# Turned attention probabilities kept tile by tile, and value matmuls that read them with a stride of 16 words

## The chip, the core and the metric

The kernel runs on one core of one Trainium2 chip. Its time is the device time of one launch in microseconds (us). The engines are TensorE (PE in the rows, its weight loads PEld), VectorE (DVE), ScalarE (ACT), GpSimd (POOL) and SyncE (SP), which issues the DMAs. SBUF has 128 partitions; PSUM is used here as eight banks of 128 partitions x 512 fp32 words.

## The reference, cut to what matters

The program is a network of eight blocks over 4 sequences (lanes) of 512 tokens and 128 features: windowed and linear attention, experts, two attentions with relative positions, two windowed attentions with rotary positions and a long convolution. The change touches the two attentions with relative positions alone. With 16 heads of 8 features they compute, for each lane:

```
att = q.k^T * scale + q.rk          (rk: a row of embk that depends on the distance t - s)
att = softmax(att)                   (the first attention is causal, the second is not)
y   = att @ v  +  einsum('bhts,tsd->bhtd', att, rv)
```

Each probability is so used twice: against the values `v` of its head, and against a table `rv` that depends on the distance alone.

## The kernel before, in words

All else being untouched, what counts is `core(s)`, written once for each engine, and run twice: `which` 0 (causal, about 775 to 1185 us of the span) and `which` 1 (not causal, about 1395 to 2085 us).

The unit of work is a tile: 8 queries (`QG`) of 16 heads (`HEADS_R`), 128 rows in order (query, head), against `nk` blocks of 128 keys. `nk` is 4 in the second attention, and 1 to 4 in the first (block of the query plus 1). There are 256 tiles in each attention, 16 tiles (one block of 128 queries) make a batch. All engines walk in steps of two tiles (`core_steps`), each part of the work at its own lag: scores at lag 6, turn at 8, embedded at 10, chosen at 12. So what a step makes is used by PE one step later, except the scores, whose softmax is used by the turn one step later as well.

For a tile:

- `scores` (PE): five or six matmuls into a bank, rows (query, head), columns keys. They are of type fp32r.
- `maxima` (DVE), `exps` (ACT), `normal` (DVE): the softmax, written to `PR`, rows (query, head).
- `turn` (PE, line 937): `nk` transposes to a bank, now rows keys, columns (block, query, head).
- `turned` (ACT, in the rows line 1166, the helper `copy`): the bank to `PT` in SBUF. `PT` has 3 slots of 8 tiles (`t.slot`); in a slot the order of words is (block, head, 64 queries), and a tile fills 8 queries in each head (`t.cols`). The copy reads its bank in order and writes word after word 64 words apart.
- `embedded` (PE): the probabilities of a tile against the table by distance, weights of 64 columns, the moving side a tile's 128 words of `PT`: 16 runs of 8 words, 64 words apart. Two matmuls run side by side, in two halves of the array's columns.
- `chosen` (DVE, line 1554): from the bank of `embedded` the words that belong to each own query, into `WB`, in order (head, query).
- `values` (PE): for a batch and each block, weights of 32 columns from `VS`, the moving side 2 slots x 64 queries of one head, in `PT` two runs of 64 words in order. Four matmuls run side by side, in four strips of the array's columns, each with another head. They are spread over 8 of the 16 tiles of a later batch.
- `fold` (PE) adds what `chosen` left, and `head_copy` (DVE) brings the batch out.

In the rows `low` is the memory that holds `PR`, `PT` and `VS`; `bank<-low` with weights of 128*32 is `values`, `bank<-low,table_low` with 128*64 is `embedded`; `halves`, `table_keys` and `exact` are operands of `scores`; `slot` holds `WB` and one of the four `PR`. Line 730 is the helper `mm`.

Of the kernel before, what the change touches and what calls it, by code (L numbers as in the profile page):

```python
# [22 lines left out]
P = 128  # L23
C = 4
T = 512
NT = T // P
# [9 lines left out]
HEADS_R, D_R, QG = 16, 8, 8  # L36
# [399 lines left out]
def hybrid_network(nc, ins, scratch, out):  # L436
    plan, released, bank_of, tile_before = make_plan()
    ctx = ExitStack()
    with ctx:
# [5 lines left out]
        def sem(name):  # L445
            if name not in sems:
                sems[name] = ctx.enter_context(nc.semaphore(name))
            return sems[name]

        bank = [ctx.enter_context(nc.psum_tensor(f"bank{b}", [P, T], F32)) for b in range(BANKS)]  # L450
# [26 lines left out]
        def carve(*shape):  # L477

            size = 1
            for s in shape:  # L480
                size *= s
            a = place[0][:, cursor[0]:cursor[0] + size]
            cursor[0] += size
            assert cursor[0] <= place[1], cursor[0]
            if len(shape) == 1:
                return a
            names = "abcd"[:len(shape)]
            return a.rearrange(f"p ({' '.join(names)}) -> p {' '.join(names)}",
                               **{n: s for n, s in zip(names[1:], shape[1:])})
# [35 lines left out]
        PR3 = carve(3, T)  # L525
        NBR, RSR, RIR = carve(4), carve(8), carve(8)
        VS = carve(NT, 4, 4, 32)
        PT = carve(3, NT, HEADS_R, QG * QG)
        cursor[0], place = 0, [halves, WORK_W - LOW]
        A4, AX4 = carve(2, 2, T), carve(2, 2, T)  # L530
        B4 = carve(2, T)
# [9 lines left out]
        WB = slots[1][:, WR_W:WR_W + 2 * HEADS_R * QG * QG].rearrange("p (a h q) -> p a h q", a=2, h=HEADS_R)  # L541
# [29 lines left out]
        def k_(name):  # L571
            a, w = CONST[name]
            return const[:, a:a + w]
# [34 lines left out]
        def reached(eng, name, count):  # L608

            if not isinstance(count, int) or count > 0:  # L610
                eng.wait_ge(sem(name), count)

        def score_columns(t):

            return t.nk * P if t.which or t.g < 4 else (t.nk - 1) * P + (t.g + 1) * QG

        def core_steps(which):

            for T_ in range(0, STEPS, 2):
                def st(work_, lag, T_=T_):
                    if 0 <= T_ - lag < TILES:
                        work_(Tile(which, T_ - lag))
                yield T_, st
# [93 lines left out]
        def _(pe):  # L721
# [7 lines left out]
            def mm(o, l, r, start=True, stop=True):  # L729
                return pe.matmul(o, l, r, start=start, stop=stop)  # L730
# [156 lines left out]
            def core(s):  # L887
# [52 lines left out]
                def embedded(t):  # L940
                    pe.wait_ge(sem("r_turn_copied"), t.at + 1)
                    reached(pe, "r_chosen", t.at - 1)
                    o = bank[4 + t.G % 2]
                    near = list(range(t.nk)) if s.which else [t.block - 1, t.block]
                    for j, b in enumerate(near):
                        apart = b - t.block
                        if b < 0:
                            rows_ = k_("zeros")
                        elif apart < -1:
                            rows_ = far_before  # L950
                        elif apart > 1:
                            rows_ = far_after
                        else:
                            first = (P * (apart + 1) + P - QG - QG * t.g) * D_R
                            rows_ = value_table[:, first:first + QG * D_R]
                        strip = slice(64 * (j % 2), 64 * (j % 2) + 64)
                        last = mm(o[strip, 0:P], rows_, PT[:, t.slot, max(b, 0), :, t.cols], start=(j < 2), stop=(j + 2 >= len(near)))
                    last.then_inc(sem("r_embedded"), 1)

                def values(T_):  # L960
                    k, part = divmod(T_ - VALUES, BATCH)
                    if not (0 <= k < BATCHES and part < QG):
                        return
                    lane, block = divmod(k, NT)
                    nk = NT if s.which else block + 1
                    two = sorted((2 * k % 3, (2 * k + 1) % 3))
                    moving = PT[:, two[0]:two[1] + 1:two[1] - two[0]]
                    steps = [(b, i) for b in range(nk) for i in range(4)]
                    if part == 0:
                        pe.wait_ge(sem("r_values_spread"), 4 * (C * s.which + lane) + 4)  # L970
                        reached(pe, "r_head_copied", BATCHES * s.which + k)
                    for b, i in steps[-(-part * len(steps) // QG):-(-(part + 1) * len(steps) // QG)]:
                        for strip in range(4):
                            last = mm(bank[7][32 * strip:32 * strip + 32, 0:P], VS[:, b, strip, i, :], moving[:, :, b, 4 * strip + i, :],
                                      start=((b, i) == steps[0]), stop=((b, i) == steps[-1]))
                        if (b, i) == steps[-1]:
                            last.then_inc(sem("r_values"), 1)
# [23 lines left out]
                for T_, st in core_steps(s.which):  # L1001
                    st(scores, SCORES)
                    st(scores, SCORES - 1)
                    st(spread, SCORES - 2)
                    st(turn, TURN)
                    st(turn, TURN - 1)
                    st(embedded, EMBED)
                    st(embedded, EMBED - 1)
                    values(T_)
                    values(T_ + 1)  # L1010
                    fold(T_)
# [148 lines left out]
        def _(act):  # L1160
# [4 lines left out]
            def copy(dst, src):  # L1165
                return act.activation(dst, src, ACT.Identity)  # L1166
# [71 lines left out]
            def core(s):  # L1238
                def turned(t):
                    act.wait_ge(sem("r_turned"), t.at + 1)  # L1240
                    m = t.G // QG
                    if t.G % QG == 0 and m >= 3:
                        act.wait_ge(sem("r_values"), BATCHES * s.which + (m - 3) // 2 + 1)
                    copy(PT[:, t.slot, 0:t.nk, :, t.cols].rearrange("p b h q -> p b q h"),
                         bank[2 + t.G % 2][:, 0:t.nk * P].rearrange("p (b q h) -> p b q h", b=t.nk, q=QG))\
                        .then_inc(sem("r_turn_copied"), 1)

                def exps(t):
                    act.wait_ge(sem("r_max"), t.at + 1)
                    n = score_columns(t)  # L1250
                    act.activation(PR[t.G % 4][:, 0:n], bank[t.G % 2][:, 0:n], ACT.Exp, bias=NBR[:, t.G % 4:t.G % 4 + 1],  # L1251
                                   accum_out=RSR[:, t.G % 8:t.G % 8 + 1]).then_inc(sem("r_exp"), 1)

                for T_, st in core_steps(s.which):
                    st(exps, SCORES)
                    st(exps, SCORES - 1)
                    st(turned, TURN)
                    st(turned, TURN - 1)
# [80 lines left out]
        def _(dve):  # L1339
# [201 lines left out]
            def core(s):  # L1541
# [7 lines left out]
                def chosen(t):  # L1549
                    half = t.G // QG % 2  # L1550
                    dve.wait_ge(sem("r_embedded"), t.at + 1)
                    if t.G % QG == 0:
                        reached(dve, "r_folded", 2 * BATCHES * s.which + 2 * (t.batch - 1) + half + 1 if t.batch else 0)
                    dve.tensor_tensor(WB[:, half, :, t.cols], bank[4 + t.G % 2][:, 0:P].rearrange("p (h q) -> p h q", h=HEADS_R),  # L1554
                                      k_("own_query").rearrange("p (h q) -> p h q", h=HEADS_R), ALU.mult)\
                        .then_inc(sem("r_chosen"), 1)

# [43 lines left out]
                for T_, st in core_steps(s.which):  # L1601
                    st(chosen, CHOSEN)
                    st(chosen, CHOSEN - 1)
                    position_copy(T_)
                    head_copy(T_)
                    st(maxima, SCORES)
                    st(maxima, SCORES - 1)
                    st(normal, SCORES)
                    st(diagonal, SCORES - 2)
                    st(normal, SCORES - 1)  # L1610
# [349 lines left out]
```

## Time and profile before

| what | value |
|---|---|
| median of 3 runs | 3362.26 us (3359.34 to 3362.66) |
| profiled execution, its own time | 3348.03 us |
| its span | 3346.1 us |
| mean granted TensorE clock | 0.963 |
| PE busy (matmuls) | 3069.0 us, 92% |
| DVE busy | 2030.3 us, 61% |
| ACT busy | 1893.0 us, 57% |
| POOL busy | 773.8 us, 23% |

The busy share of PE counts a matmul to its modelled end, and matmuls overlap, so it is not a measure of what the array can do. The pace of PE is read from how many instructions lie in a stretch, and its idle time from the view of waits.

### The profile page before, as it was taken

The numbers are of one execution on the slowest core, as the hardware profiler recorded it, in microseconds if no ns is written. First come the engines' busy times: TensorE is split into PE (matmuls) and PEld (weight loads), VectorE is DVE, ScalarE is ACT, GpSimd is POOL, SyncE is SP. The second block draws the span as 40 slices with busy tenths as digits, with TensorE's granted clock in tenths as the row PEclk, the third lists the DMA queues.
The fourth block names the chain that finished last, engine by engine and source line by source line (L and its number), as shares of the span: only waits on it lengthen the run. The fifth ranks groups of instructions, "written<-read, shape, count | busy, mean of one in ns | idle before, by whom it ended". The sixth has DMA issues, their size and how long they took to land. (4 is left out here: it accounts for less than half of the span.)

```text
span 3346.1 us, 61245 instructions
## 1 busy us (share of the span) xinstructions
PE 3069.0 (92%) x22620; PEld 2079.8 (62%) x22620; DVE 2030.3 (61%) x6331; ACT 1893.0 (57%) x4388; POOL 773.8 (23%) x683
## 2 busy tenths in 40 slices
PE   8999999978999998799999999888888998888888
PEld 6666667546888885488888887344344463443444
DVE  5454535366677675666666666667566425774765
ACT  5464656514666663266666665666565615665665
POOL 1000000102233230244444442221222012212220
PEclk9898999988999998899999999899999999999999
DMA  1010000000000001000000000210111002111110
GB/s 48 1 37 1 11 1 8 1 4 8 2 2 2 2 2 30 21 2 2 2 1 2 2 2 28 88 39 20 41 39 29 20 1 58 38 27 27 41 36 13
DMA packets 34537, 61.57 MB, mean 18 GB/s; under 512 B 11182, under 2 KB 15302, under 8 KB 33094
## 3 DMA queue, kind: packets, MB, share of 16 engines
q1 hardware_dynamic: 34246, 57.65, 6.3%
q8 instruction: 187, 3.06, 0.4%
q14 instruction: 104, 0.85, 0.1%
HBM read 21.97 MB, written 1.11 MB: 7 GB/s over the span
## 5 line engine op out<-in xcount | busy, mean ns | idle before, releaser
L730 PE MATMUL bank<-work 128*64 128x128 f32 (+8 forms) x4992 | 581.5, 302 | 65.5 <-DVE work L1649 36.0
L730 PEld LDWEIGHTS bank<-work 128*64 128x64 f32 (+3 forms) x4992 | 426.1, 165 | 261.6 <-issue 162.9
L1569 DVE TENSOR_REDUCE low<-bank 128x1 f32<-128x512 f32 (+22 forms) x512 | 293.6, 574 | 294.8 <-PE bank L730 293.1
L1251 ACT ACTIVATE low<-bank,low 128x512 f32<-128x512 f32 (+23 forms) x384 | 227.9, 594 | 395.9 <-DVE low L1569 394.9
L1166 ACT ACTIVATE low<-bank 128x512 f32<-128x512 f32 (+3 forms) x512 | 424.0, 938 | 0.9 <-PE bank L937 0.9
L730 PE MATMUL bank<-table_keys,halves 128*128 128x512 f32 (+3 forms) x1536 | 418.2, 381 | 0.2 <-ACT low L1251 0.2
L1283 ACT ACTIVATE work<-work 128x192 f32<-128x192 f32 (+1 forms) x512 | 221.4, 436 | 263.9 <-DVE work L1636 263.4
L1166 ACT ACTIVATE work<-bank 128x512 f32<-128x512 f32 (+4 forms) x469 | 262.0, 577 | 137.2 <-PE bank L730 54.2
L1796 POOL TENSOR_TENSOR work<-work 128x512 f32<-128x512 f32 x128 | 164.0, 1281 | 595.5 <-DMA work<-work 593.7
L730 PEld LDWEIGHTS bank<-table_keys,halves 128*128 128x128 f32 x1536 | 253.2, 192 | 68.6 <-issue 34.6
L730 PE MATMUL bank<-halves 128*128 128x512 f32 (+3 forms) x1024 | 286.8, 362 | 1.0 <-DVE halves L1562 0.9
L1757 POOL TENSOR_TENSOR halves<-squared,const 128x512 fp32r<-128x512 f32 x128 | 135.6, 1059 | 650.1 <-PE bank L730 650.1
L1717 POOL TENSOR_SCALAR normed<-normed,slot 128x512 f32<-128x512 f32 x48 | 78.6, 1637 | 736.2 <-DVE normed L1394 735.9
L730 PE MATMUL bank<-work,slot 128*128 128x512 f32 x408 | 198.7, 622 | 34.1 <-ACT work L1166 29.2
L730 PE MATMUL bank<-low,table_low 128*64 128x128 f32 x2944 | 225.0, 281 | 0.3 <-DVE slot L1554 0.3
L1170 ACT ACTIVATE squared<-centered 128x512 f32<-128x512 f32 x80 | 50.1, 630 | 287.7 <-DVE centered L1387 287.6
L730 PE MATMUL bank<-normed,slot 128*128 128x512 f32 x440 | 206.8, 613 | 1.7 <-POOL normed L1717 1.7
L730 PE MATMUL bank<-centered,const 128*128 128x512 f32 x256 | 146.9, 656 | 65.9 <-ACT centered L1264 65.1
L730 PEld LDWEIGHTS bank<-halves 128*128 128x128 f32 x1024 | 184.9, 191 | 31.3 <-DVE halves L1562 3.2
L1547 DVE TENSOR_SCALAR low<-low 128x512 f32<-128x512 f32 (+23 forms) x384 | 191.2, 498 | 13.6
L1049 PEld LDWEIGHTS bank<-const,work 128*128 128x128 f32 x896 | 111.6, 145 | 127.8 <-issue 104.1
L730 PEld LDWEIGHTS bank<-low,table_low 128*64 128x64 f32 x2944 | 162.9, 136 | 38.0 <-issue 37.9
(182 smaller groups left out, 5601.7 us busy)
## 6 DMA issues: line engine op xcount, KB each, us to landing
work<-work SPq DMA_DIRECT2D x512, 64.0 KB, 2.0
slot<-in_wW SPq DMA_DIRECT2D x4, 1605.5 KB, 7.0
slot<-in_wA SPq DMA_DIRECT2D x4, 837.0 KB, 6.3
table_low<-embv_padded SPq DMA_DIRECT2D x2, 1536.0 KB, 6.3
table<-in_dft SPq DMA_DIRECT2D x1, 3072.0 KB, 11.7
slot<-in_wE SPq DMA_DIRECT2D x2, 584.0 KB, 3.7
const<-in_const SPq DMA_DIRECT2D x1, 1094.0 KB, 5.1
squared<-in_x SPq DMA_DIRECT2D x4, 256.0 KB, 6.2
```

The costliest lines, as they stand in the source:

```text
L730: return pe.matmul(o, l, r, start=start, stop=stop)
L1049: last = pe.transpose(o[:, (2 * a + blk) * P:(2 * a + blk + 1) * P], PW[:, s.n % 3, a, blk * P:(blk + 1) * P], ident)
L1166: return act.activation(dst, src, ACT.Identity)
L1170: act.activation(squared[:, s.c, :], centered[:, s.c, :], ACT.Square).then_inc(sem("norm_squared"), 1)
L1251: act.activation(PR[t.G % 4][:, 0:n], bank[t.G % 2][:, 0:n], ACT.Exp, bias=NBR[:, t.G % 4:t.G % 4 + 1], accum_out=RSR[:, t.G % 8:t.G % 8 + ...
L1283: last = act.activation(PW[:, s.n % 3, a, lo:256], SW[:, s.n % 2, a, lo:256], ACT.Exp, scale=-1.0, bias=small_w[:, s.n % 4, a:a + 1], accu ...
L1547: dve.tensor_scalar(row, row, inverse, None, ALU.mult).then_inc(sem("r_normal"), 1)
L1569: dve.tensor_reduce(out=NBR[:, t.G % 4:t.G % 4 + 1], in_=bank[t.G % 2][:, 0:score_columns(t)], axis=AX.X, op=ALU.max, negate=True).then_in ...
L1717: pool.tensor_scalar(a, a, wt(s, s.table, s.gain[1]), None, ALU.add).then_inc(sem("norm_done"), 1)
L1757: pool.tensor_tensor(A4[:, half, Q % 2, :].rearrange("p (t h) -> p t h", h=HEADS_R), bc(one_lane.unsqueeze(2), [P, 4 * QG, HEADS_R]), bc(k ...
L1796: pool.tensor_tensor(R1[:, s.n % 3, :], R1[:, s.n % 3, :], R2[:, s.n % 3, :], ALU.add).then_inc(sem("w_added"), 1)
```

## The change

`PT` is laid out anew: a slot is now (tile of the 8, block, 128 words as the turn gives them, in order (query, head)). The ACT copy thus reads and writes in order. `embedded` reads 128 words in order, and its result comes in order (query, head), so `chosen` reads its bank with a stride of 16 words and writes `WB` as before. `values` needs one head of 2 x 64 queries: it reads 128 words that lie 16 words apart (in 8 tiles for each slot, 8 words each). The sizes of all operands, the waits and the order of the instructions on each engine stay as they were.

```diff
-        PT = carve(3, NT, HEADS_R, QG * QG)
+        PT = carve(3, QG, NT, P)
...
-                        last = mm(o[strip, 0:P], rows_, PT[:, t.slot, max(b, 0), :, t.cols], start=(j < 2), stop=(j + 2 >= len(near)))
+                        last = mm(o[strip, 0:P], rows_, PT[:, t.slot, t.G % QG, max(b, 0), :], start=(j < 2), stop=(j + 2 >= len(near)))
...
-                    moving = PT[:, two[0]:two[1] + 1:two[1] - two[0]]
+                    slots_ = slice(two[0], two[1] + 1, two[1] - two[0])
...
-                            last = mm(bank[7][32 * strip:32 * strip + 32, 0:P], VS[:, b, strip, i, :], moving[:, :, b, 4 * strip + i, :],
+                            last = mm(bank[7][32 * strip:32 * strip + 32, 0:P], VS[:, b, strip, i, :], PT[:, slots_, :, b, 4 * strip + i:P:HEADS_R],
...
-                    copy(PT[:, t.slot, 0:t.nk, :, t.cols].rearrange("p b h q -> p b q h"),
-                         bank[2 + t.G % 2][:, 0:t.nk * P].rearrange("p (b q h) -> p b q h", b=t.nk, q=QG))\
+                    copy(PT[:, t.slot, t.G % QG, 0:t.nk, :].rearrange("p b f -> p (b f)"), bank[2 + t.G % 2][:, 0:t.nk * P])\
...
-                    dve.tensor_tensor(WB[:, half, :, t.cols], bank[4 + t.G % 2][:, 0:P].rearrange("p (h q) -> p h q", h=HEADS_R),
+                    dve.tensor_tensor(WB[:, half, :, t.cols], bank[4 + t.G % 2][:, 0:P].rearrange("p (q h) -> p h q", h=HEADS_R),
                                       k_("own_query").rearrange("p (h q) -> p h q", h=HEADS_R), ALU.mult)\
```

## Rows read from the trace of the kernel before

**Rows 1.** The page, busy time of each engine

```profile
PE 3069.0 (92%) x22620; PEld 2079.8 (62%) x22620; DVE 2030.3 (61%) x6331; ACT 1893.0 (57%) x4388; POOL 773.8 (23%) x683
```

**Rows 2.** Windows: stretch, its us, busy time of each engine, granted clock

```profile
920.00:1046.00 126.00, 125.77 (x1466) 106.03 (x1460) 89.14 (x288) 77.76 (x198) 36.48 (x37) 1.00 0.01 2
1570.00:1740.00 170.00, 170.00 (x1895) 138.77 (x1894) 114.31 (x311) 111.08 (x193) 80.81 (x70) 1.00 0.01 2
```

**Rows 3.** PE's waits from 1395 to 2085 us: total, times, longest

```profile
PE bank L730 <- POOL halves L1757: 11.4, 1, 11.4
PE bank L937 <- ACT low L1166: 1.0, 2, 0.7
PE bank L730 <- DVE centered L1598: 0.5, 1, 0.5
PE bank L730 <- ACT low L1251: 0.2, 1, 0.2
```

**Rows 4.** Timeline of a steady stretch: start, us, engine, operation [idle before]

```profile
1701.71 0.85 PE L730 MATMUL bank<-table_keys,halves 128*128 128x512 f32 x3
1701.91 0.69 DVE L1569 TENSOR_REDUCE low<-bank 128x1 f32<-128x512 f32 x1 [0.63 <-PE bank L730]
...
1702.40 0.62 PE L730 MATMUL bank<-halves 128*128 128x512 f32 x2
1702.63 0.42 PEld L730 LDWEIGHTS bank<-halves,exact 128*128 128x128 f32 x2
1702.63 0.69 ACT L1251 ACTIVATE low<-bank,low 128x512 f32<-128x512 f32 x1 [0.57 <-DVE low L1569]
1702.86 0.63 PE L730 MATMUL bank<-halves,exact 128*128 128x512 f32 x2
...
1703.33 1.04 PE L937 MATMUL bank<-const,low 128*128 128x128 f32 x8
...
1704.29 1.09 PE L730 MATMUL bank<-low,table_low 128*64 128x128 f32 x16
...
1704.46 1.98 ACT L1166 ACTIVATE low<-bank 128x512 f32<-128x512 f32 x2
```

**Rows 5.** Groups by form, ACT's copies: count | busy us, mean ns | idle

```profile
L1166 ACT ACTIVATE low<-bank 128x512 f32<-128x512 f32 x320 | 319.7, 1110 | 0.0
...
L1166 ACT ACTIVATE low<-bank 128x384 f32<-128x384 f32 x64 | 49.8, 887 | 0.0
L1166 ACT ACTIVATE work<-bank 128x512 f32<-128x512 f32 x345 | 196.5, 590 | 56.2 <-PE bank L1121 30.6 <-PE bank L827 11.6 <-PE bank L1049 7.7
L1166 ACT ACTIVATE low<-bank 128x256 f32<-128x256 f32 x64 | 34.8, 652 | 0.0
L1166 ACT ACTIVATE low<-bank 128x128 f32<-128x128 f32 x64 | 19.7, 413 | 0.9 <-PE bank L937 0.9
...
L1166 ACT ACTIVATE work<-bank 128x256 f32<-128x256 f32 x16 | 5.8, 360 | 0.0
```

**Rows 6.** Line 1166: who waited for its copies, us and times

```profile
  PE bank L937: 2.4, 4
```

**Rows 7.** Timeline of the second attention's end

```profile
2075.28 3.78 ACT L1166 ACTIVATE low<-bank 128x512 f32<-128x512 f32 x4
2075.41 0.16 DVE L1546 RECIPROCAL low<-low 128x1 f32<-128x1 f32 x1 [0.25 <-ACT slot L1251]
2075.61 0.49 DVE L1547 TENSOR_SCALAR slot<-slot,low 128x512 f32<-128x512 f32 x1
...
2076.46 0.63 PE L937 MATMUL bank<-const,low 128*128 128x128 f32 x4 [0.72 <-ACT low L1166]
...
2077.35 0.63 PE L937 MATMUL bank<-const,slot 128*128 128x128 f32 x4 [0.26 <-ACT low L1166]
...
2077.91 2.24 PE L730 MATMUL bank<-low,table_low 128*64 128x128 f32 x32
...
2080.07 1.96 PE L730 MATMUL bank<-low 128*32 128x128 f32 x64
```

**Rows 8.** Line 730, matmuls of values: count, ns min/median/max

```profile
L730 PE MATMUL bank<-low x3328: 272/273/298, 815.2 to 2083.9; 128*32 128x128 f32 x196
```

**Rows 9.** Groups by form, DVE from 780 to 2090 us

```profile
L1554 DVE TENSOR_TENSOR slot<-bank,const 128x128 f32<-128x128 f32 x512 | 123.0, 279 | 5.4 <-PE bank L730 4.8
...
L1596 DVE COPY centered<-bank 128x128 f32<-128x128 f32 x11 | 3.1, 283 | 5.5 <-PE bank L730 5.5
```

## The prediction

> **What bounds the kernel now.** I read the page first: PE is busy for 92% of the span, ACT for 57% [rows 1]. That is a mean over stages, so the windows come next, of the two stages that the change touches. In a steady stretch of the second attention PE is busy for 170.00 of 170.00 us, DVE for 114.31, ACT for 111.08; in the first attention (920 to 1046 us) it is 125.77, 89.14 and 77.76 of 126 [rows 2]. PE's clock is granted in full (2.4 GHz) in both. A busy PE could still be one that overlaps modelled ends with small waits, so I look at its waits: in the whole second attention it waits 11.4 us once for POOL at the start, and 1.7 us in all beside that, 1.0 us of it for the ACT copies that the change makes shorter [rows 3]. The reader is to see that no line of these is a wait in the steady part. So in both attentions the time is the sum of what PE's instructions take, and ACT and DVE run beside it with a third of their time idle.
>
> The timeline of a step shows that this holds by a wide margin. The copies of a step's turned tiles run from 1704.46 to 1706.44 [rows 4], and their reader (`embedded` at lag 10) comes one step later, some five us on. DVE idles 0.63 us before the first maximum, ACT 0.57 us before the exponential [rows 4].
>
> **The ACT copies.** There are 512: 320 of 512 words at 1110 ns, and 64 each of 384, 256 and 128 words at 887, 652 and 413 ns [rows 5]. The same helper with both sides in order takes 590 ns for 512 words and 360 ns for 256 (two runs of 128) [rows 5]. That is 0.90 ns a word, and by it 475 ns for 384 and 245 ns for 128. The saving on ACT is 320 x 0.520 + 64 x (0.412 + 0.292 + 0.168) = 166 + 56 = 222 us. It is large, and nearly all of it lies beside PE. On the path lies only what PE waits for: 2.4 us in four places over both attentions [rows 6]. At the end of the second the timeline tells why. No more scores come, PE has little to do, and the turn needs the bank that the copy of two tiles before still reads: 0.72 and 0.26 us [rows 7]. Four copies in a row take 3.78 us there, with 590 ns each about 2.4; the last turn then starts near 2076.5 instead of 2077.35. I take 1 us for each attention, 2 us in all, from 0 to 2.5.
>
> **`embedded`.** It reads 128 words in order in place of 16 runs of 8. Sixteen instructions, in eight pairs, take 1.09 us, so the pairs follow each other in (1.09 - 0.27)/7 = 0.117 us, where 0.27 is the length of the last. The eight transposes, which read 128 words in order, one at a time, take 1.04 us, (1.04 - 0.27)/7 = 0.110 us [rows 4]. The pace is nearly the same, so runs of 8 cost little or nothing before. Were the rest of 7 x 0.007 = 0.05 us due to them, 256 steps of two tiles would give back 13 us. But it can as well be the wait for the first weights of a new width, as `values`, in order, also starts with 0.113 for 0.110 (below). I take 0, from 0 to -13.
>
> **`chosen`.** 512 DVE instructions of 279 ns [rows 9] now read their bank with a stride of 16 words. A plain copy of the same size with both sides in order takes 283 ns [rows 9], so the runs of 8 that it writes cost nothing today; the strided read is not in the trace. If each of the 128 words cost as much more as ACT's strided writes do (next part: 0.92 ns), one would take 0.12 us longer, 0.24 us in a step of two tiles; the 0.63 us of idle time before the next maximum [rows 4] covers it. Behind it on DVE are the maximum, the reciprocal and the scaling, and PE needs those one step later. I take 0; below it nothing is to be had, and with the cover gone at every step it would be 256 x 0.24 = 61 us, which I hold for very unlikely since the turn has the better part of a step of slack.
>
> **`values`.** This alone is on PE's own path. There are 3328 instructions [rows 8], four side by side, so 832 rounds of 128 words for each strip. From the row of 64 (16 rounds) in 1.96 us [rows 7]: (1.96 - 0.27)/15 = 0.113 us a round, 94 us over both attentions. After the change each stream takes a word from a new place at every step. No matmul of this kernel does that today, so I bound it from both sides.
> - Below: reading in order is no slower than anything else of this type here, so there is no gain; 0.
> - For free: PE's reading has room. The fp32r matmuls of `scores` start at 1701.71 and the sixth at 1702.86 [rows 4], 0.230 us for 512 words, 0.45 ns a word. The fp32 matmuls take 0.113/128 = 0.88 ns a word. So the stream that is to be strided runs at half of the pace that the same engine reaches in order, and a penalty of up to two would be hidden.
> - Like ACT: its writes with 64 words between them cost (1110 - 413)/384 = 1.82 ns a word, in order (590 - 360)/256 = 0.90 [rows 5]. If PE's read paid 1.82 ns too, a round would take 128 x 1.82 = 0.233 us, 0.120 more: 832 x 0.120 = +100 us.
> - The far end: four streams read side by side. If what they share hands out several neighbouring words at once, words in order need one fetch for four, and strided words one fetch each. A round would take four times as long, 0.339 us more: +282 us.
>
> I take the free case, 0, for `values`: the row of fp32r is of the same engine and the same side (a read), that of ACT is a write by another engine.
>
> The Trainium skill speaks against this change. SBUF — State Buffer, on cachelines in its part on the ports, says that SBUF has lines of 16 bytes, that two accesses to a line are needed for full bandwidth, and that each access to a new line pays a penalty; here every word is on a line of its own. What the penalty is it does not say. The doubled cost of ACT's strided words agrees with it. No row shows a strided read by PE. If the penalty is a halving of the best pace of the engine, an estimate from that rule and the fp32r rows is 0.90 ns a word, 2 us in all, and the sum stays; if it is a fixed time for each line it is rival 1.
>
> **Sum.** -2 (ends) + 0 + 0 + 0 = -2 us. In the profiled execution 3348.0 becomes 3346.0; the median of the runs, 14 us above it, becomes 3360.3. A difference of 0.2%, 6.7 us, is about what a measurement of this kernel can tell from none.
>
> **Rivals.**
> 1. *Each strided word costs PE a fixed time like ACT's.* Place: the 832 rounds of `values`, price 0.120 us each, 3362 + 100 - 2 = 3460 us. It decides as soon as a word costs over 0.88 ns. For it: ACT's 1.82 ns, and the skill's rule. Against it: ACT's is a write. It would be seen in full, since PE has no idle time to hide it in. Between nothing and this lie smaller penalties (a round of 0.12 to 0.18 us), 6 to 60 us.
> 2. *The four strips share their fetches.* 3362 + 282 - 2 = 3642 us. For it: four streams in order keep the pace of one, which could be luck of neighbouring words. Against it: `embedded` with two streams in short runs shows nothing of it, at the same pace as the transposes [rows 4].
> 3. *ACT was the hidden bound, or its strided writes held PE up,* and over 6.7 us come back: half of ACT's 222 us would make 3251, the 13 us of `embedded` alone 3347. Against it: PE waits 2.4 us in all for these copies [rows 6], and while the two copies run from 1704.46 on, PE's matmuls keep their pace. Beyond those 13 us I see no way.
>
> **Chances.** The free case 0.46; small penalties of 6 to 60 us 0.08; rival 1 0.29; rival 2 0.11; rival 3 0.06. Of the free case a hundredth lies past 0.2%. From these: faster 0.06, same 0.45, slower 0.49. The likeliest single case is the free one, 3360.5 us, with a range of its own of 3355 to 3366. For 8 in 10 the range must take in rival 1 with some spread: 3355 to 3480. Left out are rival 2, the upper tail of rival 1 and a real gain.
>
> **What would show each step.** In the profile after, the copies of 512 words take 590 to 600 ns and ACT's busy time falls by about 220 us. PE's waits for line 1166 shrink from 2.4 us to nearly none. A row of 64 matmuls of `values` takes 1.96 us again; 3.8 us would be rival 1, about 7 rival 2. The matmuls of `embedded` keep 1.09 us for 16. `chosen` takes 279 to 400 ns, with no wait of PE for it. I am wrong if the row of `values` is longer, or if a wait for DVE shows up before the turns.

## The result, and the profile after

The changed kernel takes 3446.39 us, median of 4 runs (3433.13 to 3450.99), beside 3360.8 us of the kernel before, median of 4. The ratio is 1.0255, 95% interval 1.023 to 1.028: slower by 86 us (77 to 94). The forecast was 3360.5 us. The time lies inside the stated range of 3355 to 3480, but the likeliest case was no change; what came is close to the time of the first rival.

The page of the changed kernel, busy time of each engine, as in [rows 1]:

```profile
PE 3169.2 (92%) x22620; PEld 2112.3 (61%) x22620; DVE 2034.6 (59%) x6331; ACT 1702.5 (49%) x4388; POOL 773.0 (22%) x683
```

ACT lost 190 us of work and PE won 100. The same stretch as the second row of [rows 2]:

```profile
1570.00:1740.00 170.00, 170.00 (x1757) 132.76 (x1757) 106.82 (x292) 75.91 (x180) 74.84 (x64) 1.00 0.01 2
```

PE is busy for all of it, at the full clock, as before, but gets through 1757 matmuls in place of 1895. That is 7% slower on PE with nothing waited for. The reader sees the loss in the count, not in the busy share. PE's waits in the second attention, which answer to [rows 3]:

```profile
PE bank L730 <- POOL halves L1756: 11.4, 1, 11.4
PE bank L730 <- DVE work L1511: 3.2, 1, 3.2
PE bank L730 <- ACT low L1250: 0.8, 2, 0.4
PE bank L730 <- DVE centered L1597: 0.5, 1, 0.5
PE bank L730 <- DVE halves L1561: 0.4, 1, 0.4
PE bank L937 <- ACT low L1166: 0.3, 1, 0.3
```

The stretch asked for, 1420 to 2190 us, takes in the end of the stage ahead (the 3.2 us, before 1450). The 11.4 us at its start are the same, and the wait for the turned copies has gone from 1.0 to 0.3 us. What is new, 0.6 us more for line 1250 and 0.4 for line 1561, is far too little for the loss. The timeline of the second attention's end, beside [rows 7]:

```profile
2177.51 0.63 PE L937 MATMUL bank<-const,low 128*128 128x128 f32 x4 [0.28 <-ACT low L1166]
2178.00 0.63 PE L937 MATMUL bank<-const,slot 128*128 128x128 f32 x4
...
2178.56 2.24 PE L730 MATMUL bank<-low,table_low 128*64 128x128 f32 x32
...
2180.73 3.66 PE L730 MATMUL bank<-low 128*32 128x128 f32 x64
```

Here stands the whole result. `embedded` takes 2.24 us for 32 as before. The 64 matmuls of `values` take 3.66 us in place of 1.96. There are 3328 / 64 = 52 such portions: 52 x 1.70 = 88 us. Line 730, beside [rows 8] (count, ns min/median/max, first and last start):

```profile
L730 PE MATMUL bank<-low x3328: 376/394/400, 833.6 to 2187.9; 128*32 128x128 f32 x196
L730 PE MATMUL bank<-low,table_low x2944: 272/273/476, 801.6 to 2180.5; 128*64 128x128 f32 x197
```

The second of these groups in the kernel before:

```profile
L730 PE MATMUL bank<-low,table_low x2944: 272/273/476, 792.4 to 2079.9; 128*64 128x128 f32 x197
```

So of the 99 us between the two profiled spans 9.2 lie ahead of the first of these matmuls, where nothing was changed, and 91.4 between the first and the last. The 9.2 us are scatter between executions: the profiled execution of the kernel before was 14 us faster than its median, and in the ten kernels of the experiments, which change nothing there either, the group starts between 795.3 and 804.9 us. The copies and `chosen`, beside [rows 5] and [rows 9] (mean ns after the busy time):

```profile
L1166 ACT ACTIVATE low<-bank 128x512 f32<-128x512 f32 x320 | 171.9, 593 | 0.6 <-PE bank L937 0.6
L1166 ACT ACTIVATE low<-bank 128x384 f32<-128x384 f32 x64 | 27.6, 486 | 0.0
L1166 ACT ACTIVATE low<-bank 128x256 f32<-128x256 f32 x64 | 20.7, 379 | 0.0
L1166 ACT ACTIVATE low<-bank 128x128 f32<-128x128 f32 x64 | 14.2, 273 | 1.7 <-PE bank L937 1.7
```

```profile
L1553 DVE TENSOR_TENSOR slot<-bank,const 128x128 f32<-128x128 f32 x512 | 123.2, 279 | 4.0 <-PE bank L730 3.1
```

The copies of 512 words take 593 ns in place of 1110, and the two of a step 1.08 us in place of the 1.98 of [rows 4]:

```profile
1743.24 1.08 ACT L1166 ACTIVATE low<-bank 128x512 f32<-128x512 f32 x2
```

Over the whole kernel the turn (line 937) waits 1.0 us for line 1166, in place of 2.4 [rows 6]. `chosen` takes 279 ns with its bank read 16 words apart, the same as in order.

### The profile page after: what moved, and what is told of

Its sections match the earlier page's. It is cut to its first block and busy times, and to the rows that moved or that the text cites. A ratio compares the mean times of both kernels' runs of the same rounds, so it can differ in the third digit from the quotient of the medians.

```text
span 3445.1 us, 61245 instructions
## 1 busy us (share of the span) xinstructions
PE 3169.2 (92%) x22620; PEld 2112.3 (61%) x22620; DVE 2034.6 (59%) x6331; ACT 1702.5 (49%) x4388; POOL 773.0 (22%) x683
## 3 DMA queue, kind: packets, MB, share of 16 engines
HBM read 21.97 MB, written 1.11 MB: 7 GB/s over the span
## 5 line engine op out<-in xcount | busy, mean ns | idle before, releaser
L1166 ACT ACTIVATE low<-bank 128x512 f32<-128x512 f32 (+3 forms) x512 | 234.4, 513 | 2.4 <-PE bank L937 2.4
L730 PE MATMUL bank<-low 128*32 128x128 f32 x3328 | 204.3, 393 | 0.0
```

## The experiments

Theory L, formed on this result: what costs is the moving side of `values` alone. A stream of words into TensorE runs at half its pace when it uses fewer than two words of a line of 4 (16 bytes), whatever runs beside it. The expectations of e4, e5 and e8 still put it as a fixed time of about 1.7 ns for each line; e8 is the run that tells a fixed time from a factor. The rivals are named in the expectations. Kernels e1 to e3 were run 6 to 12 times each, the others once, so that what e4 to e10 say rests on their rows and not on their totals. In the comparisons below "row of 32" is 32 matmuls of `values` in one step, eight rounds of four, in order 1.08 us.

**Which part of the change costs.** Two kernels divide it.

```diff
 e1_in_order, against the changed kernel
-    VS[:, b, strip, i, :], PT[:, slots_, :, b, 4 * strip + i:P:HEADS_R],
+    j = 4 * strip + i
+    VS[:, b, strip, i, :], PT[:, slots_, j // 2, b, 64 * (j % 2):64 * (j % 2) + 64],
```

> The changed kernel, but each matmul of values reads two runs of 64 neighbouring words of the same slots in place of 128 words 16 apart, so that it multiplies other probabilities than it should. Theory L (each strided word of the values reads costs TensorE time, and nothing else of the change matters): the time of before less the 2 us of the ends, 3358 us, a row of 32 matmuls of values 1.04 us in place of 1.93. Rival O (the in-order copies or the strided read of chosen also cost something): slower than before by over 7 us. Rival G (the in-order reads of embedded give something back): 3347 us, 13 us under before.

```diff
 e2_stride_alone, against the kernel before
-    VS[:, b, strip, i, :], moving[:, :, b, 4 * strip + i, :],
+    words = moving[:, :, b].rearrange("p a h q -> p a (h q)")[:, :, 4 * strip + i:QG * P:HEADS_R]
+    VS[:, b, strip, i, :], words,
```

> The kernel before, with the old layout, the old copies, embedded and chosen; only the matmuls of values read 128 words 16 apart in the old slots (other probabilities than they should). Theory L: the whole loss is here, 832 rounds x 0.107 us = 89 us, so 3449 us. Rival O: clearly less than that, since part of the loss came from the rest of the change. A round should last 0.220 us.

Measured: e1 3358.4 us, ratio 0.9995 (0.9977 to 1.0014); e2 3449.49 us, ratio 1.0264 (1.0241 to 1.0288). Timelines, of e1 and then of e2 (start, us, engine, operation):

```profile
1803.55 1.09 PE L730 MATMUL bank<-low,table_low 128*64 128x128 f32 x16
1804.58 1.08 PE L730 MATMUL bank<-low 128*32 128x128 f32 x32
```

```profile
1819.54 1.09 PE L730 MATMUL bank<-low,table_low 128*64 128x128 f32 x16
1820.57 1.93 PE L730 MATMUL bank<-low 128*32 128x128 f32 x32
```

The stride alone, in the old kernel with its slow copies, costs the whole 2.6%. All the rest of the change, with ACT's 190 us, is worth nothing that can be measured (e1: between 8 us less and 5 us more). So the 13 us of rival G, from the reads of `embedded`, do not come back either.

**Where ACT's own loss was.** The old layout, the same words to the same places, the copy walked in the other order.

```diff
 e3_runs_of_8, against the kernel before
-    copy(PT[:, t.slot, 0:t.nk, :, t.cols].rearrange("p b h q -> p b q h"),
-         bank[2 + t.G % 2][:, 0:t.nk * P].rearrange("p (b q h) -> p b q h", b=t.nk, q=QG))
+    copy(PT[:, t.slot, 0:t.nk, :, t.cols],
+         bank[2 + t.G % 2][:, 0:t.nk * P].rearrange("p (b q h) -> p b h q", b=t.nk, q=QG))
```

> The kernel before with its layout, the same words to the same places, but ACT walks through the copy in the other order: it reads its bank 16 words apart and writes runs of 8 neighbouring words. Theory L with ACT's loss on the writes' side: a copy of 512 words 590 to 600 ns, values reads in order, time 3358 us (2 us under before, not to be told from it). Rival: ACT pays for the strided read of the bank as it did for the strided write, 1110 ns a copy, 3360 us.

Measured: 3360.97 us, ratio 1.0007 (0.9994 to 1.002). Its copies by form:

```profile
L1166 ACT ACTIVATE low<-bank 128x512 f32<-128x512 f32 x320 | 172.1, 593 | 0.6 <-PE bank L937 0.6
```

The full saving on ACT is so to be had with one line and without a strided read on PE. ACT reads its bank 16 words apart at no cost and pays only for scattered single words on the side that it writes. As the forecast said of the saving, it buys no time here.

**Which strides cost.** Only the words that `values` reads differ.

```diff
 e4_stride_2_and_4 and e5_pairs_and_8, against the changed kernel (j = 4 * strip + i)
-    PT[:, slots_, :, b, 4 * strip + i:P:HEADS_R]
+    e4, first attention:  PT[:, slots_, j // 2, b, j % 2:P:2]
+    e4, second:           PT[:, slots_, 2 * (j // 4):2 * (j // 4) + 2, b, j % 4:P:4]
+    e5, first attention:  PT[:, two[0], :, b, :].rearrange("p t (q r w) -> p t q r w", q=QG, w=2)[:, :, :, j % 8, :]
+    e5, second:           PT[:, slots_, 4 * (j // 8):4 * (j // 8) + 4, b, j % 8:P:8]
```

> The changed kernel with other strides of the values reads (other probabilities than it should): 2 words in the first attention, 4 words in the second. Theory L as lines of 4 words, a fetch of 1.72 ns each: a round at stride 2 0.110 to 0.113 us (two words a fetch), at stride 4 0.220 us as at 16. Rival S (any step but 1 halves the pace): 0.220 us at both. Rival D (the distance of 64 bytes matters): 0.113 us at both. Time by theory L 3360 + 512 rounds x 0.107 = 3415 us, by rival S 3449, by rival D 3360.

> The changed kernel with other words for the values reads (other probabilities than it should): in the first attention pairs of two neighbouring words, the pairs 16 words apart; in the second single words 8 apart. Theory L (a stream pays about 1.7 ns for each line of 4 words that it enters, and 0.85 ns for each word at least): pairs 0.110 to 0.115 us a round, stride 8 0.217 to 0.229 us. Rival S (any gap costs a fixed time): pairs about 0.165 us.

e4 took 3408.84 us and e5 3426.79. Rows of e4, at stride 2 and at stride 4:

```profile
1161.21 1.13 PE L730 MATMUL bank<-low 128*32 128x128 f32 x32
...
1822.40 2.03 PE L730 MATMUL bank<-low 128*32 128x128 f32 x32
```

Rows of e5, pairs 16 words apart and single words 8 apart:

```profile
1176.52 1.09 PE L730 MATMUL bank<-low 128*32 128x128 f32 x32
...
1804.97 2.04 PE L730 MATMUL bank<-low 128*32 128x128 f32 x32
```

A gap as such is free: pairs 16 words apart run as fast as words in order (1.09 us), a stride of 2 nearly so (1.13). From a stride of 4 words on, where each word is alone in its 16 bytes, the time doubles; at strides of 4 and 8 a round takes (2.03 - 0.41)/7 = 0.23 us, a little more than the 0.217 to 0.229 that the expectations had. The rivals that any step or only the distance of 64 bytes counts have fallen. The totals are 11 us below and 7 us above what the rows give (3358 + 512 x 0.12 = 3419); a single run does not tell that from scatter.

**Alone or shared among the four streams.**

```diff
 e6_strips, against the changed kernel
+    words = (the words of e1) if strip > s.which else (the words of the change)
 e7_one_stream, against the changed kernel
+    if strip and (b, i) not in (steps[0], steps[-1]):
+        continue
+    words = (the words of the change) if s.which else (the words of e1)
```

> The changed kernel, values with a mix (other probabilities than it should): in the first attention one of the four strips reads 16 words apart and three read in order, in the second two and two. Theory L, each stream limited by itself: the four move together, so a round is 0.217 us in both. Rival Q (the four streams share a number of fetches, and 4 x 128 fetches take 0.217 us): with one strided stream 128 + 3 x 32 = 224 fetches of 512, so 0.11 us (the floor); with two 320, 0.136 us.

> The changed kernel with three of the four strips of values left out except in the first and last step of a batch (most of the heads' values are missing), in order in the first attention, 16 words apart in the second. Theory L: a single stream takes 0.109 us for 128 words in order and 0.217 us with the stride. Rival Q: 0.109 us in both, since a single stream makes only a quarter of the fetches.

e6 took 3451.31 us and e7 3412.45. Rows of e6, one strip of four strided, then two:

```profile
1073.21 1.92 PE L730 MATMUL bank<-low 128*32 128x128 f32 x32
...
1817.09 1.92 PE L730 MATMUL bank<-low 128*32 128x128 f32 x32
```

Rows of e7, eight matmuls of a single stream (the other three strips are left out), in order and strided:

```profile
1060.28 1.06 PE L730 MATMUL bank<-low 128*32 128x128 f32 x8
...
1842.53 1.90 PE L730 MATMUL bank<-low 128*32 128x128 f32 x8
```

One strided stream of four is as slow as four (1.92 us). One stream all by itself shows the same doubling: (1.90 - 0.39) / 7 = 0.216 us for 128 words. So nothing is shared out among the streams; each has its pace, and the slowest holds the round. Rival Q has fallen, and with it rival 2 of the prediction.

**A fixed time for a line, or a factor.** The other type of matmul tells these apart, since its stream runs twice as fast in order. `values` reads in order here.

```diff
 e8_fp32r, against e1_in_order: step = 8 if s.which else 4
-    mm(o[:, 0:t.nk * P], A4[:, half, Q % 2, mine], keys_[:, t.lane, 0:t.nk * P],
+    mm(o[:, 0:t.nk * P], A4[:, half, Q % 2, mine], (table_keys, from word 0, or 2048 for KR_LO in the first attention)[:, 0:t.nk * P * step:step],
```

> The changed kernel with values read in order, and the first three matmuls of scores (fp32r, 512 words of keys in 0.230 us in order, 0.45 ns a word) read keys 4 words apart in the first attention and 8 apart in the second (scores of other keys than they should be). Theory L with a fixed time for each line: 512 x 1.7 = 0.87 us a matmul, four times the present one; in the second attention 768 matmuls x 0.64 = 490 us more. Rival P (the stride halves what the type of matmul reaches in order): 0.46 us, 768 x 0.23 = 177 us more.

Measured: 3606.95 us. A step of its timeline, in the second attention:

```profile
1853.33 1.54 PE L730 MATMUL bank<-table_keys,halves 128*128 128x512 f32 x3
1854.69 0.65 PE L730 MATMUL bank<-halves 128*128 128x512 f32 x2
1855.18 1.46 PE L730 MATMUL bank<-table_keys,halves 128*128 128x512 f32 x3
1856.46 0.65 PE L730 MATMUL bank<-halves 128*128 128x512 f32 x2
```

Three strided matmuls of 512 words go from 1855.18 to 1856.46, 0.427 us each, 0.83 ns a word; in [rows 4] it is 0.230 us, 0.45 ns a word. A fixed 1.7 ns for each line would have given 0.87 us. It is a factor of 1.86, nearly two as in fp32, so rival P holds and the fixed time has fallen. In the first attention, at stride 4, it is the same: three take 1.39 us (1195.07 to 1196.46), 0.463 us each, where the kernel before takes 0.75 (1134.35 to 1135.10), 0.25 each.

```profile
1195.07 1.58 PE L730 MATMUL bank<-table_keys,halves 128*128 128x512 f32 x3
1196.46 0.65 PE L730 MATMUL bank<-halves 128*128 128x512 f32 x2
```

```profile
1134.35 0.91 PE L730 MATMUL bank<-table_keys,halves 128*128 128x512 f32 x3
1135.10 0.64 PE L730 MATMUL bank<-halves 128*128 128x512 f32 x2
```

The price of 177 us was for the second attention alone; by the rows it is 768 x 0.197 = 151 us there, and the first attention, which the expectation left out, makes most of the rest of the 249. Words in pairs were not tried in fp32r.

**The weights' side, two streams, and a stride of 3.**

```diff
 e9_weights, against e1_in_order
-    VS[:, b, strip, i, :]
+    flat = VS[:, b].rearrange("p s i d -> p (s i d)")
+    flat[:, j:512:16] if s.which else flat[:, 128 * strip + i:128 * strip + 128:4]
 e10_embedded_4, against e1_in_order, second attention only
-    embedded: PT[:, t.slot, t.G % QG, max(b, 0), :]
+    embedded: PT[:, t.slot, t.G % QG].rearrange("p b f -> p (b f)")[:, b::4]
+    values:   PT[:, two[0], j // 2].rearrange("p b f -> p (b f)")[:, j % 2:384:3]
```

> The changed kernel with values' moving words in order, but their weights (32 words of VS for each load) read with a stride: 4 words in the first attention, 16 in the second (other weights than they should be). Theory L applied to the loads as well: a load reads at half pace too. If the load stays hidden beside the matmul before it, a round stays at 0.109 us and the time at 3358 us; if not, a round grows to at most 0.217 us and the time to at most 3447 us.

> The changed kernel, first attention with all of its reads in order. In the second, embedded (two streams side by side) reads 128 words 4 apart, and values 128 words 3 apart (other probabilities than they should). Theory L: the pairs of embedded follow at 0.217 to 0.23 us instead of 0.109, so 16 matmuls take about 1.9 us instead of 1.09 and 128 steps x 0.85 = 110 us are lost; values, whose lines of 4 words are hit once or twice in turn, lie between, 0.15 to 0.18 us a round (512 rounds, 20 to 36 us). Time 3490 to 3505 us. Rival (it is a matter of four streams): embedded keeps 1.09 us.

e9 took 3362.61 us, and its row of 32 in the second attention is

```profile
1804.03 1.11 PE L730 MATMUL bank<-low 128*32 128x128 f32 x32
```

The weight loads of `values`, of e1 and then of e9 (ns min/median/max):

```profile
L730 PEld LDWEIGHTS bank<-low x3328: 106/110/110, 831.1 to 2097.7; 128*32 128x32 f32 x196
```

```profile
L730 PEld LDWEIGHTS bank<-low x3328: 131/136/161, 830.8 to 2098.5; 128*32 128x32 f32 x196
```

The loads grew from 110 to 136 ns, but stay hidden; the row is 0.03 us longer. e10 took 3512.0 us. Its rows of `embedded` at stride 4 and `values` at stride 3:

```profile
1802.79 2.03 PE L730 MATMUL bank<-low,table_low 128*64 128x128 f32 x16
1804.74 1.57 PE L730 MATMUL bank<-low 128*32 128x128 f32 x32
```

Two streams pay like four and like one: 0.94 us for 16 matmuls, where the expectation had 0.85. A stride of 3, with one or two words in a line, lies between (1.57). 128 x 0.94 + 64 x 0.49 = 152 us on top of 3358 make 3510; measured 3512, and so 7 us above the 3490 to 3505 that were expected.

## Why the prediction was wrong

- *PE bounds both attentions, ACT and DVE run beside it:* right. It is why the loss came through in full. e1 and e3 take 190 us from ACT and change nothing that can be measured.
- *The ACT copies, 222 us saved, 2 on the path:* the sizes of the copies were right to 30 ns (593, 486, 379, 273), ACT's busy time fell by 190.5 us. The 222 us overstated it, since the busy time of these copies went from 424.0 us to 234.4. Of the 32 us too many, 28 come from multiplying the mean time of one copy by the count. Two copies in a row overlap: two of 1110 ns take 1.98 us [rows 4], two of 593 take 1.08 in the changed kernel. So one copy of 512 words frees (319.7 - 171.9) / 320 = 0.46 us of ACT, not 0.52. The sizes account for the other 4 us. PE's waits for these copies fell from 2.4 to 1.0 us, less than the 2 us taken; neither can be seen in e1 (0.9977 to 1.0014). The sum itself gives 3360.3, not 3360.5, which changes nothing.
- *`embedded`, 0:* right, 1.09 us for 16 before and after. Of the 13 us at its far end nothing came.
- *`chosen`, 0:* right, and for a simpler reason than the idle time that was to cover it: it takes 279 ns either way.
- *`values`, 0:* this is the step that failed: a strided read was put at no cost, in the words "the stream that is to be strided runs at half of the pace that the same engine reaches in order, and a penalty of up to two would be hidden". The penalty is close to two. But it is not taken from the best pace of the engine: each type of matmul is halved from its own. fp32r goes from 0.230 to 0.427 us for 512 words (e8), fp32 from 0.113 to 0.216 for 128 (e7). Room that one type shows is no room in the other. By these paces a word of fp32 costs twice a word of fp32r, in order (0.88 and 0.45 ns) and strided (1.69 and 0.83); this would be so if an fp32 matmul read each word twice at fp32r's pace, which is argued and not shown. Measured, the term is 832 x (0.218 - 0.113) = 87 us, where 0.218 is (3.66 - 0.39) / 15 from the row of 64.
- *Rival 1* had place and bound right (832 rounds, no idle time to hide in), and its price nearly, 0.120 for 0.105 us a round. Its mechanism, a fixed time like ACT's, was wrong: e8 would have taken 0.9 us a matmul. That its price was so near is luck: ACT's copies in order (0.90 ns a word) and PE's fp32 matmuls in order (0.88) happen to have the same pace, and both come to about twice that with scattered words (1.82 and 1.69). Whether ACT's writes double for the same reason as PE's reads was not tried.
- *Rival 2* (shared fetches) and *rival 3* (ACT the hidden bound, or a gain in `embedded`) have both fallen, the one by e7, the other by e1 and e3.
- *The rule of the Trainium skill* (SBUF — State Buffer, the passage on cachelines of 16 bytes and two hits in each) was weighed and then discounted. These runs agree closely with its two hits in a line, by the rows of 32 (in order 1.08): 1.09 and 1.13 us where a line gives two words, 1.57 where it gives one or two, 1.93 to 2.04 where it gives one. A penalty for each new line as such, which the passage also has, does not show: the pairs 16 words apart change line at every pair and run as in order. The estimate of 0.90 ns a word from it was wrong by nearly two, as it took the best pace of fp32r for that of fp32.
- *Chances:* slower had 0.49 and no change 0.45. One result can't tell whether these were put right. The range held the time because it was stretched to take in rival 1, whose price came out near for another reason; that is partly luck.

What stays open: strides of 4 and 8 words (2.03, 2.04 us) are a little slower than 16 (1.93). No run was made to tell why. Nor is it shown why fp32 takes twice the time of fp32r for a word, or why its penalty comes on top of that.

## What to carry to other kernels

Before a stride is moved from one engine to another, ask which of them has idle time. Here 0.46 us in each copy of 512 words on ACT, idle for a third of the time, was traded for 0.1 us in each round on PE, which hardly ever waits in this stage. Lay out the moving side of a matmul so that it takes at least two fp32 words from each 16 bytes; gaps between such pairs cost nothing here (pairs 16 words apart). Where a scattered copy is slow, try first to walk it in the other order, so that the strided side is the PSUM read and the writes come in short runs.

## What the hardware showed that was not expected

- The penalty of a moving side with one word in each 16 bytes is a factor of nearly two in both types: 0.113 to 0.216 us for 128 fp32 words, 0.230 to 0.427 us for 512 fp32r words.
- A single strided stream in four holds the other three at its pace (1.92 us for 32 in e6, 1.93 with four).
- Reading a PSUM bank 16 words apart costs nothing on DVE (279 ns for 128 words in both) and nothing on ACT (593 ns for 512 words), while ACT's writes of single words 64 apart take 1110 ns, and its writes in runs of 8 take 593.
- Strided weights make a load of 32 words 26 ns longer, hidden beside the matmuls (row of 32: 1.11 us for 1.08).
